# Two attention layers and a mixture of experts: batch 0's tokens sorted by expert, and the causal mask of the row maxima moved to VectorE

## The chip, the core and the metric

The kernel runs on one core of a Trainium2 chip. The metric is the device time of one execution in microseconds (us), the median of several. The engines are named as the profile names them: PE is TensorE (PEld its weight loads), DVE is VectorE, ACT is ScalarE, POOL is GpSimd, SP is SyncE, which issues most of the DMAs. PSUM is the memory that PE writes to, in 8 banks of 128 rows x 512 float32 columns.

## The reference

Input x is (2, 1024, 128) in float32: 2 batches of 1024 tokens, in the kernel 16 tiles of 128 tokens, 8 per batch. Cut to what matters:

```python
x = layernorm(x + attention8(x))         # 8 heads of 16, causal, plus a rank-1 term per head in the scores
n = rmsnorm(x); x = x + mla_attention16(n)   # 16 heads of 8, rotated q and k, keys/values from a 64-wide latent, causal
n = rmsnorm(x)
top = argmax(n @ gate_w.T + gate_b)      # one of 4 experts per token
h = relu(n @ W1[e].T + b1[e])            # 128 -> 512, computed for all e
y = h @ W2[e].T + b2[e]                  # 512 -> 128
x = x + y[top]                           # the chosen expert's result alone
out = layernorm(x)
```

## The kernel before

**Attention** runs in 12 groups of 4 heads: groups 0 to 3 are layer 0 (two per batch), 4 to 11 are layer 1 (four per batch). Keys and queries of a group are bf16 products stacked along the rows. For layer 0 a head uses all 128 rows of the array; for layer 1 it uses 64, and heads 0, 1 and 2, 3 lie in different halves, so that matmuls of the two halves can run at once. A softmax needs each row's maximum before its exponentials, so scores are computed twice. First, for the maxima, with queries as output rows: `MAXES` lists 40 units per group, each a row block i against up to 512 keys, one head, or two where they fit in one bank. `maxima` (L1156) writes a unit to one of 3 banks in a ring (`MAXN`), and DVE reduces the bank to one maximum per row (L1604), after which PE may use it again. 24 of the 40 units hold the diagonal. For these PE first writes the mask into the last 128 columns of each head: a matmul of an identity with a tile of 0 and -1e30 (L1178 in layer 0; L1184 and L1186, 128 and 64 columns wide, in layer 1), and then adds the scores to it (L1189). The maxima are combined, transposed, split into three bf16 parts (L1485 to L1500) and carried by SP into the last rows of the queries (L967, L973), so that the second pass of scores (L1210), with keys as output rows, has the maximum subtracted in it. ACT takes the exponential (L1382), POOL zeroes what lies above the diagonal (L1083, 8 times per group), PE multiplies by the values in float32 (L1227), with 4 buffers of probabilities (`PSLOTS`). A group has 40 units of exponentials too.

**Experts.** A block is 512 tokens, (b, i) with i = 0, 1. After layer 1's attention of a block come the normalised tokens `hat` (L1136), their transpose `feat` (L1394), the gate and `pick` (L1566), which leaves a one-hot row per token. Then all 4 experts are computed for all tokens: 16 `hidden` matmuls of 512 columns (L1362), a `relu` each (L1458), 4 bias matmuls (L1302), 64 `expert` matmuls of 128 columns (L1306), and DVE adds each expert's result times the one-hot column (L1685). All in float32; the profile records each float32 matmul as two. A block thus has 32 records of L1362 and 128 of L1306.

**The order of work** is made once by a planner in Python (`order`, L507). Every step has a wanted position in units of groups (`FIRST`, `BETWEEN`, `READY`, `EXPERTS`, `RESULTS`, L269 to L273), a list of what it needs (`needs`), and costs on each engine (`COSTS`, L312). The planner emits one list, `SCHEDULE`, and each engine runs its own steps of it in that order, in order. Batch 0's two expert blocks are wanted at positions 7.9 to 11.4, beside attention groups 8 to 11; batch 1's at 11.6 to 14.0, for the most part after attention. POOL's and SP's DMAs stand in the same order: a wait in front of one holds what follows on that queue.

## Time and profile before

| | |
|---|---|
| median of 3 runs | 613.81 us (613.73 to 614.38) |
| the profiled execution | 617.44 us |
| its span, first to last instruction | 615.7 us |
| mean granted clock of PE | 0.955 of full speed |
| DMA | 25.64 MB, mean 42 GB/s |

The page says how long each engine was busy in the profiled execution, which chain of work ended last, and which groups of instructions cost most. In its slices the granted clock of PE dips several times in the first half (to 0.5 in a stretch) and stays at nine tenths or more from about 310 us to almost the end. A busy PE is not PE at its peak: matmuls overlap, and the end of one is modelled. So durations of a matmul are longer than the distance from one to the next.

In the rows of a stretch the columns are: start and end in us, length, then busy us and instructions in parentheses for PE, PEld, DVE, ACT, POOL (or for the one engine asked for), then PE's granted clock, the DMA engines' mean busy share and GB/s. In the rows of a group of instructions: line, engine, operation, output<-inputs, shapes, count | busy us, mean ns of one | idle us of the engine before them, and who ended it. In the rows of the timeline: start us, us to the end of the last, engine, line, operation, shapes, and how many were merged.

### The profile page before, as it was taken

How to read it: one execution, taken by the hardware profiler on the slowest of the kernel's cores; microseconds unless marked ns; L12 is line 12 of the kernel's file. 1: busy time of each engine (PE TensorE's matmuls, PEld its weight loads, DVE VectorE, ACT ScalarE, POOL GpSimd, SP SyncE). 2: the span in 40 equal slices, each digit the busy share in tenths (PEclk: the TensorE clock that was granted, in tenths of full speed). 3: DMA queues.
4: the chain of work that ended last, by engine and by line, in shares of the span. 5: the costliest groups of instructions: out<-in, count | busy, mean ns of one | idle time of the engine just before them, and what ended most of it. 6: DMA issues, size and time to landing. Idle time of an engine off the chain costs nothing.

```text
span 615.7 us, 10700 instructions
## 1 busy us (share of the span) xinstructions
PE 549.5 (89%) x3869; PEld 255.0 (41%) x3885; DVE 416.2 (68%) x1063; ACT 350.7 (57%) x673; POOL 157.3 (26%) x217
## 2 busy tenths in 40 slices
PE   6577799888899988898989999999999999999993
PEld 3323234434433333332333334543545445347662
DVE  4396989768888869786878887776666721643144
ACT  4413267754765767745767776656556666653330
POOL 9631012353534155342111221301101102201000
PEclk9877899997999999996989999999999999999998
DMA  3992023005022001020010101001000000010000
GB/s 117 178 210 91 21 70 104 2 1 200 17 71 62 1 25 56 26 79 28 2 54 2 53 2 54 2 2 53 2 3 2 1 2 1 2 35 2 0 15 20
DMA packets 27846, 25.64 MB, mean 42 GB/s; under 512 B 7377, under 2 KB 24401, under 8 KB 27538
## 3 DMA queue, kind: packets, MB, share of 16 engines
q1 hardware_dynamic: 27410, 24.17, 14.4%
q0 software_dynamic: 384, 0.79, 0.7%
q8 instruction: 31, 0.51, 0.3%
q14 instruction: 21, 0.17, 0.1%
HBM read 17.30 MB, written 7.34 MB: 40 GB/s over the span
## 4 chain that ended last, share of the span: by engine, by line
PE 69%; DVE 8%; SPq 8%; ACT 7%; DMA 3%; issue 3%; POOL 1%; DVEq 0%; ACTq 0%; POOLq 0%
PE ps L1227 15%; PE ps L1210 12%; PE ps L1306 10%; PE ps L1362 10%; PE ps L1189 9%; ACT pr L1382 5%; DVE mparts L1604 4%; SPq L913 4%; PE ps L1292 3%; SPq L967 2%; PE ps L1286 2%; DMA qs<-nparts 2%; PE ps L1238 2%; PE ps L1267 2%; PE ps L1184 1%
## 5 line engine op out<-in xcount | busy, mean ns | idle before, releaser
L1382 ACT ACTIVATE pr<-ps 128x512 f32<-128x512 f32 (+1 forms) x480 | 249.9, 554 | 167.1 <-PE ps L1210 137.0
L1604 DVE TENSOR_REDUCE mparts<-ps 128x1 f32<-128x512 f32 (+3 forms) x480 | 279.9, 630 | 89.1 <-PE ps L1189 87.5
L1210 PE MATMUL ps<-qs,ks 64*128 64x512 bf16 (+7 forms) x560 | 153.3, 338 | 18.3 <-ACT pr L1382 10.1
L1189 PE MATMUL ps<-ks,qs 61*128 61x512 bf16 (+7 forms) x576 | 155.4, 347 | 6.9 <-DMA qs<-nparts 3.7
L1227 PE MATMUL ps<-pr,vs 128*32 128x512 f32 (+3 forms) x1152 | 125.0, 507 | 1.5 <-ACT pr L1382 0.3
L1083 POOL TENSOR_SCALAR_AFFINE_SELECT pr<-pr 128x512 f32<-128x512 f32 x96 | 60.9, 634 | 227.7 <-ACT pr L1382 227.6
L1210 PEld LDWEIGHTS ps<-qs,ks 64*128 64x128 bf16 (+1 forms) x576 | 44.6, 96 | 136.9 <-ACT pr L1382 97.5
L1306 PE MATMUL ps<-w,work 128*128 128x128 f32 x512 | 67.7, 283 | 0.0
L1189 PEld LDWEIGHTS ps<-ks,qs 61*128 61x128 bf16 (+1 forms) x576 | 51.0, 100 | 37.8 <-DVE mparts L1604 19.6
L1362 PE MATMUL ps<-feat,w 128*128 128x512 f32 x128 | 65.8, 621 | 0.0
L1306 PEld LDWEIGHTS ps<-w,work 128*128 128x128 f32 x512 | 60.2, 191 | 9.5 <-issue 9.3
L1458 ACT ACTIVATE work<-ps,b 128x512 f32<-128x512 f32 x64 | 43.6, 687 | 32.2 <-PE ps L1362 31.6
L1227 PEld LDWEIGHTS ps<-pr,vs 128*32 128x32 f32 x1152 | 23.0, 108 | 38.6 <-issue 30.2
L1178 PE MATMUL ps<-cmask,identb 128*128 128x128 bf16 (+1 forms) x96 | 25.2, 264 | 14.5 <-DMA ks<-scr0k 6.6
L1685 DVE SCALAR_TENSOR_TENSOR xn<-ps,onehot,xn 128x128 f32<-128x128 f32 x48 | 13.5, 343 | 25.8 <-PE ps L1306 25.8
L1507 DVE RECIPROCAL rc<-ps 128x16 f32<-128x16 f32 x24 | 6.0, 251 | 35.7 <-PE ps L1238 35.7
L1362 PEld LDWEIGHTS ps<-feat,w 128*128 128x128 f32 x128 | 20.6, 189 | 17.6 <-issue 14.8
L1184 PE MATMUL ps<-cmaskx,identx 64*128 64x128 bf16 (+1 forms) x96 | 23.5, 245 | 0.8 <-DVE mparts L1604 0.7
L1184 PE MATMUL ps<-cmask,identb 64*128 64x128 bf16 (+1 forms) x96 | 23.4, 244 | 0.8 <-DVE att L1511 0.4
L1077 POOL COPY vs<-vall 128x256 f32<-128x256 f32 (+1 forms) x12 | 6.0, 502 | 69.5 <-PE ps L1227 69.4
L1178 PEld LDWEIGHTS ps<-cmask,identb 128*128 128x128 bf16 x96 | 9.9, 104 | 31.9 <-DVE mparts L1604 21.8
L1186 PE MATMUL ps<-cmaskx,identx 64*128 64x64 bf16 (+1 forms) x96 | 19.3, 201 | 0.0
(138 smaller groups left out, 501.3 us busy)
## 6 DMA issues: line engine op xcount, KB each, us to landing
qs<-scr0q SPq DMA_DIRECT2D x48, 64.0 KB, 2.3
qs<-scr1q SPq DMA_DIRECT2D x84, 32.0 KB
ks<-scr1k SPq DMA_DIRECT2D x84, 32.0 KB
ks<-scr0k SPq DMA_DIRECT2D x36, 64.0 KB, 2.2
scr0q<-parts SPq DMA_DIRECT2D x4, 384.0 KB, 2.9
scr0k<-parts SPq DMA_DIRECT2D x4, 384.0 KB, 3.8
scr1q<-parts SPq DMA_DIRECT2D x4, 384.0 KB, 2.6
scr1k<-parts SPq DMA_DIRECT2D x4, 384.0 KB, 2.6
```

Source lines behind the costliest of these rows:

```text
L913: queue.dma_start(to, src.rearrange("(h d) t -> d h t", d=at.hd)).then_inc(k_first[half] if (F, k) == (0, 1) else qk_in[F % SLOTS][half % ...
L1083: pool.affine_select(out=p, in_=p, compare_op=ALU.is_ge, fill=0.0, base=0, pattern=[[0, HG], [1, P]], channel_multiplier=-1).then_inc(done ...
L1178: pe.matmul(bank[:, :, w - P:w], identb[:, :], cmask[:, 0:nh, :], start=True, stop=False, skip_group_check=True)
L1184: pe.matmul(bank[:, :, w - P:w], low[0][own, :], low[1][own, 0:nh, :], start=True, stop=False, skip_group_check=True)
L1189: last = pe.matmul(bank[:, h, :], queries(F, 0, h0 + h, i * P, P), keys(F, 0, h0 + h, 512 * c, w), start=not diagonal, stop=True, skip_gro ...
L1210: last = pe.matmul(to[:, h, :], keys(F, 3, h0 + h, j * P, P), queries(F, 3, h0 + h, qb * 512 + lo, n), start=True, stop=True)
L1227: last = pe.matmul(ps[VW * h:VW * (h + 1), PVB, lo:lo + n], vs[:, F % VSLOTS, j, VW * h:VW * (h + 1)], pr[:, st % PSLOTS, h, 0:n], start=( ...
L1306: last = pe.matmul(to, hid[:, e % 2, c, t * P:(t + 1) * P], w2[:, e * HC + c, :], start=False, stop=(c == HC - 1), skip_group_check=True)
L1362: pe.matmul(side(*step), w1[:, c * P:(c + 1) * P], feat[:, columns(b, i)], start=True, stop=True).then_inc(done["hidden"], 1)
L1382: act.activation(pr[:, st % PSLOTS, h0:h0 + nh, 0:STEPS[st][3]], scores_at(F, v), ACT.Exp, scale=GROUPS[F][0].scale).then_inc(exped, 1)
L1458: act.activation(hid[:, c // HC % 2, c % HC, :], side("hidden", b, i, c), ACT.Relu, bias=b1[:, c:c + 1]).then_inc(done["relu"], 1)
L1604: dve.tensor_reduce(mparts[:, F % SLOTS, h0:h0 + nh, i, c], maxes_at(F, u), AX_X, ALU.max).then_inc(taken, 1)
```

## The change

Two edits are made together.

**Sorted tokens.** For batch 0 (`SORTED = [(0, (0, 1))]`) the dense expert steps are gone. PE ranks the tokens: a matmul with a strict lower-triangle matrix, and 8 with a matrix of ones, count for each token and expert how many came before (`rank`). DVE turns the counts into a place for each token, such that each expert's tokens start at a multiple of 128 (`places`); 1024 tokens and 4 experts need at most eleven tiles of 128. POOL scatters the 8 tiles of `hat` to these places in DRAM by indirect DMA (`scatter`), SP loads them back in pieces of four tiles (`sorted`). For each of the eleven tiles POOL fetches the weights of its expert with two indirect DMAs, 128 rows of 640 and of 516 floats (`fetch`), into two pairs of buffers that earlier steps have left free (`parts`, `cos`, `sin`); PE transposes the tile, ACT copies and scales it (`row_turn`, `row_feat`), PE makes the 4 hidden matmuls of 128 columns, ACT 4 relus of 128 columns, PE 4 output matmuls, DVE adds the bias, and SP stores the tile (`tile_hidden`, `tile_relu`, `tile_out`, `tile_sum`, `tile_store`). Then POOL gathers the tokens' rows by 8 indirect DMAs (`collect`) and DVE adds them to the residual (`collected`, one add of 512 columns per block). Batch 1 stays dense.

**The mask.** PE's mask matmuls and their tiles are gone (`identb`, `identx`, the second mask tile). DVE adds a 512-column mask tile, whose last 128 columns hold the triangle, and takes the maximum in one instruction, `tensor_tensor_reduce`, for each head of a diagonal unit, with the masked scores written back to the bank. Units without the diagonal are reduced as before.

```diff
+SORTED = [(0, (0, 1))]
+PIECES = 4
+def by_rows(s):
+    n, J = len(tokens_of(s)), rows_of_tiles(s)
+    out = [("rank", s), ("places", s)] + [("scatter", s, t) for t in range(n)]
+    out += [("fetch", s, j, w) for j in range(2) for w in range(2)]
+    out += [("sorted", s, p) for p in range(-(-J // PIECES))]
+    for j in range(J):
+        out += [("row_turn", s, j), ("row_feat", s, j), ("tile_hidden", s, j), ("tile_relu", s, j), ("tile_out", s, j),
+                ("tile_sum", s, j), ("tile_store", s, j)]
+        if j + 2 < J:
+            out += [("fetch", s, j + 2, w) for w in range(2)]
+    out += [("collect", s, t) for t in range(n)]
+    return out + [("collected", SORTED[s][0], i) for i in SORTED[s][1]]
...
-            add("result", spread(experts(b, i), *EXPERTS[b][i]))
+            if (b, i) in DENSE:
+                add("result", spread(experts(b, i), *EXPERTS[b][i]))
+    for s in range(len(SORTED)):
+        add("rows", spread(by_rows(s), *BY_ROWS[s]))
+BY_ROWS = [(8.45, 11.5)]
...
-        masked = (512 * c + w == (i + 1) * P) * nh * (128 if GROUPS[step[1]][0].n == 0 else 192)
-        return [(PE, (masked + nh * w) / 2400 + 0.01 * nh), (DVE, 0.1 + nh * w / 880)]
+        reads = nh if 512 * c + w == (i + 1) * P else 1
+        return [(PE, nh * w / 2400 + 0.01 * nh), (DVE, 0.1 * reads + nh * w / 880)]
...
+                any_rows = a["x"].rearrange("b t c -> (b t) c")[0:P * (TB + E - 1), :]
+                sp.dma_start(rows_in_order[:, :], any_rows).then_inc(rows_set, 16)
...
+            def scatter(s, t):
+                if t == 0:
+                    pool.wait_ge(rows_set, 32)
+                    pool.wait_ge(done["places"], nth("places", s))
+                b, blocks = SORTED[s]
+                pool.wait_ge(done["hat"], nth("hat", b, blocks[t // 4]))
+                pool.indirect_dma_start(rows_in_order[:, :], IndirectOffsetOnAxis(ap=place_of[:, t:t + 1], axis=0),
+                                        xn[:, tokens_of(s)[t], :], None).then_inc(scattered, 16)
+            def fetch(s, j, w):
...
+                if j >= 2 and w == 0:
+                    pool.wait_ge(done["tile_sum"], nth("tile_sum", s, j - 2))
+                to = (cos, sin)[j % 2][:, 0:w2_row] if w else fetched_w1[:, j % 2 * w1_row:(j % 2 + 1) * w1_row]
+                pool.indirect_dma_start(to, None, a[("w1_rows", "w2_rows")[w]],
+                                        IndirectOffsetOnAxis(ap=row_of[:, j:j + 1], axis=0)).then_inc(fetched[j % 2], 16)
...
-                diagonal = 512 * c + w == (i + 1) * P
-                if diagonal and GROUPS[F][0].n == 0:
-                    pe.matmul(bank[:, :, w - P:w], identb[:, :], cmask[:, 0:nh, :], start=True, stop=False,
-                              skip_group_check=True)
-                elif diagonal:
...
                 for h in range(nh):
                     last = pe.matmul(bank[:, h, :], queries(F, 0, h0 + h, i * P, P),
                                      keys(F, 0, h0 + h, 512 * c, w),
-                                     start=not diagonal, stop=True, skip_group_check=True)
+                                     start=True, stop=True)
...
+                elif kind == "tile_hidden":
+                    s, j = args
+                    pe.wait_ge(done["row_feat"], nth("row_feat", s, j))
+                    pe.wait_ge(fetched[j % 2], 32 * (j // 2 + 1))
+                    wait_bank(*step)
+                    for c in range(HC):
+                        first = j % 2 * w1_row + c * P
+                        last = pe.matmul(side(*step)[:, c * P:(c + 1) * P], fetched_w1[:, first:first + P], tile_x[:, j % 2, :],
+                                         start=True, stop=True)
...
-                    dve.tensor_reduce(mparts[:, F % SLOTS, h0:h0 + nh, i, c], maxes_at(F, u),
-                                      AX_X, ALU.max).then_inc(taken, 1)
+                    bank, to = maxes_at(F, u), mparts[:, F % SLOTS, h0:h0 + nh, i, c]
+                    if 512 * c + w < (i + 1) * P:
+                        last = dve.tensor_reduce(to, bank, AX_X, ALU.max)
+                    else:
+                        for h in range(nh):
+                            last = dve.tensor_tensor_reduce(bank[:, h, :], bank[:, h, :], cmask[:, 512 - w:512], 1.0, -3.0e38,
+                                                            ALU.add, ALU.max, to[:, h:h + 1])
+                    last.then_inc(taken, 1)
```

## Rows read from the trace of the kernel before

**Rows 1.** the page, part 1: busy time of each engine, its share, instructions
```profile
PE 549.5 (89%) x3869; PEld 255.0 (41%) x3885; DVE 416.2 (68%) x1063; ACT 350.7 (57%) x673; POOL 157.3 (26%) x217
```

**Rows 2.** the page, part 4: the chain that ended last, by line
```profile
PE ps L1227 15%; PE ps L1210 12%; PE ps L1306 10%; PE ps L1362 10%; PE ps L1189 9%; ACT pr L1382 5%; DVE mparts L1604 4%; SPq L913 4%; PE ps L1292 3%; SPq L967 2%; PE ps L1286 2%; DMA qs<-nparts 2%; PE ps L1238 2%; PE ps L1267 2%; PE ps L11
```

**Rows 3.** busy time of each engine by stretch; stretches are attention groups 5, 6, 9, 11
```profile
280.60:310.50 29.90, 26.85 (x237) 9.79 (x235) 23.75 (x46) 20.87 (x42) 5.07 (x8) 0.89 0.03 9
...
310.50:340.20 29.70, 27.62 (x250) 9.96 (x249) 24.33 (x49) 21.02 (x42) 5.51 (x9) 0.94 0.10 28
...
417.20:463.80 46.60, 46.60 (x355) 21.24 (x355) 29.77 (x62) 27.17 (x51) 5.51 (x9) 1.00 0.06 18
...
506.60:541.80 35.20, 33.35 (x239) 15.90 (x240) 14.45 (x67) 24.52 (x48) 7.38 (x10) 1.00 0.03 9
```

**Rows 4.** the same view: stretch A, stretch B, tail
```profile
50.00:340.20 290.20, 259.21 (x1878) 104.92 (x1891) 236.00 (x571) 181.14 (x361) 91.18 (x118) 0.94 0.15 46
...
340.20:541.80 201.60, 196.30 (x1512) 90.91 (x1511) 128.68 (x323) 131.34 (x252) 33.96 (x50) 1.00 0.05 15
...
541.80:615.70 73.90, 64.26 (x362) 42.88 (x360) 26.10 (x123) 23.45 (x36) 2.31 (x2) 0.97 0.04 12
```

**Rows 5.** who waited for whom in stretch A: us in total, times, longest
```profile
DVE mparts L1604 <- PE ps L1189: 46.2, 62, 3.8
```

**Rows 6.** timeline of TensorE in the tail: start us, us, instruction, count
```profile
545.46 0.59 PE L1362 MATMUL ps<-feat,w 128*128 128x512 f32 x1
...
546.30 2.94 PE L1306 MATMUL ps<-w,work 128*128 128x128 f32 x24
...
555.00 1.88 PE L1362 MATMUL ps<-feat,w 128*128 128x512 f32 x4
```

**Rows 7.** timeline in group 9: mask matmuls of one diagonal unit
```profile
441.67 0.22 PE L1184 MATMUL ps<-cmask,identb 64*128 64x128 bf16 x1
...
441.73 0.19 PE L1186 MATMUL ps<-cmaskx,identx 64*128 64x64 bf16 x1
```

**Rows 8.** instruction groups of ACT and DVE, whole trace
```profile
L1458 ACT ACTIVATE work<-ps,b 128x512 f32<-128x512 f32 x64 | 43.6, 687 | 32.2 <-PE ps L1362 31.6
...
L1430 ACT COPY work<-ps 128x256 f32<-128x256 f32 x4 | 1.5, 370 | 1.2 <-PE ps L1292 1.2
...
L1443 ACT ACTIVATE work<-work,shift,rstd 128x64 f32<-128x64 f32 x16 | 5.7, 436 | 0.0
...
L1685 DVE SCALAR_TENSOR_TENSOR xn<-ps,onehot,xn 128x128 f32<-128x128 f32 x48 | 13.5, 343 | 25.8 <-PE ps L1306 25.8
```

**Rows 9.** instruction groups by shape, whole trace, L1604
```profile
L1604 DVE TENSOR_REDUCE mparts<-ps 128x2 f32<-128x512 f32 x48 | 32.3, 685 | 8.2 <-PE ps L1189 8.0
...
L1604 DVE TENSOR_REDUCE mparts<-ps 128x2 f32<-128x256 f32 x48 | 18.7, 419 | 10.9 <-PE ps L1189 10.7
```

**Rows 10.** DVE in the timeline, back to back, and a group of small operations
```profile
308.14 1.89 DVE L1604 TENSOR_REDUCE mparts<-ps 128x1 f32<-128x512 f32 x3 [0.80 <-PE ps L1189]
...
541.52 0.38 DVE L1519 BATCH_NORM_AGGREGATE mv<-stats 128x2 f32<-128x6 f32 x4
...
L1546 DVE SCALAR_TENSOR_TENSOR rstd<-rstd 128x4 f32<-128x4 f32 (+1 forms) x48 | 7.8, 163 | 1.6
```

**Rows 11.** POOL's DMA and longest operation; landings of two DMAs
```profile
L913 POOL DMA_DIRECT2D ks<-scr0k x12 | 6.3, 531 | 8.1 <-DMA scr0k<-parts 7.8 <-POOL qs L1031 0.3
...
L1031 POOL MEMSET qs<- 32x2048 f32 x3 | 5.4, 1809 | 0.0
...
ks<-scr0k POOLq DMA_DIRECT2D x12, 64.0 KB, 4.2
...
w<-in_W2T SPq DMA_DIRECT2D x1, 1024.0 KB, 6.9
```

**Rows 12.** DVE in L1604 alone, stretches A and B
```profile
50.00:340.20 290.20, 176.65 (x306) 0.94 0.15 46
...
340.20:541.80 201.60, 90.12 (x150) 1.00 0.05 15
```

312 lines of the change are left out of this document (251 added, 61 removed).

## The prediction

> **What bounds the kernel now.** I read the page's busy shares first. TensorE is busy for 549.5 of 615.7 us, DVE for 416.2, ACT for 350.7 [rows 1]: one engine leads, but a busy TensorE is not yet a bound. The chain that ended last says the same in another way [rows 2]: its five largest parts are TensorE's, and both expert matmuls (L1306 and L1362) are among them with 10% each.
>
> Then I cut the time at the first exponential of each attention group. Groups 5 and 6, which have no expert work beside them, take 29.9 and 29.7 us; group 9, with the same attention work and batch 0's experts, takes 46.6 us with TensorE busy for all of it, DVE for 64% [rows 3]. So in the last third the experts set the pace. In groups 5 and 6 no engine is full: TensorE 0.93, DVE 0.82, ACT 0.71 of group 6. They hold each other up in turns. In the first long stretch TensorE is at 0.89, DVE at 0.81; in the second at 0.97 and 0.64; the tail after attention is batch 1's experts [rows 4]. The waits of the first stretch go both ways: DVE waits 46.2 us for the matmuls of the maxima [rows 5], and TensorE cannot write a fourth bank of maxima before DVE has read the first.
>
> **The sum is by stretch**: opening (to 50 us), A (50 to 340.2), B (340.2 to 541.8), tail (73.9 us). The profiled execution took 617.44 us, 3.6 more than the median 613.81.
>
> **Batch 0's dense experts go, from B.** Consecutive records of L1362 start 0.43 us apart ((1.88 - 0.59) / 3, with 0.59 for the last one alone), those of L1306 0.115 us ((2.94 - 0.29) / 23) [rows 6]. Half of the 128 and 512 records are batch 0's, and 8 bias matmuls of 512 bf16 columns, for which I take four times the 128-column one of rows 7: 64 x 0.43 = 27.5, 256 x 0.115 = 29.4, 8 x 0.24 = 1.9, together 58.8 us. **The eleven tiles come**: each has 4 hidden and 4 output matmuls of 128 columns, 16 records at 0.115 = 1.84, and one transpose, priced like one such record: 11 x 1.95 = 21.5; the rank's 9 short matmuls add 0.7. Net on TensorE: -36.6 us.
>
> **ACT**: 32 relus of 0.687 go (22.0 us). 44 relus and 11 copies of 128 columns come. No row has 128 columns out of PSUM with a pointer operand; a 256-column PSUM copy takes 0.370, a 64-column form with pointers 0.436 [rows 8]. I take 0.40: 22.0 us, net 0 (bounds -2 and +2). **DVE**: 32 pick-ups of 0.343, overlapping, are 9 us; new are 11 tile sums like them, two 512-column adds, priced like a reduction (0.685) [rows 9], and about 15 small operations at 0.163 [rows 10]: 3.8 + 1.4 + 2.4 = 7.6 us, net -1.4.
>
> **POOL and the queues.** POOL gets 38 indirect DMAs: 8 scatters, 22 fetches, 8 gathers. The nearest row, a plain POOL DMA, takes 0.53 us to issue and 4.2 us to land [rows 11]. At 0.53 they cost 20 us of POOL, which is busy for only 34 us of B [rows 4]; the upper bound I take is 1.8 us, as long as POOL's longest memset [rows 11]. A mask queued behind a fetch pair is 1 to 3.6 us late, which the four buffers of probabilities cover mostly: four steps ahead, ACT goes on. SP gets 3 loads and 11 stores in B, and in A, behind the expert weights, a small constant and a 0.7 MB copy that fills the sorted rows once; POOL trades the mask's second tiles for two all-ones tiles, which is even; a store waits for its tile sum, and the maxima's rows queue behind it on SP. The plan makes maxima a group ahead, so that wait is covered by some 30 us. The wait of a fetch is on the tile sum two tiles earlier, so a pair of tiles needs two issues 1.1 + landing 4.2 + hidden 0.9 + relus 1.6 + output 0.9 + sum 0.3 = 9 us, some 12 with queueing. 5.5 pairs are 66 us and the plan spreads them over three groups, 90 us. Cost 0; the cover is B's length.
>
> **The mask leaves TensorE.** In the timeline a 128-column mask matmul occupies 0.06 us up to the next; the 64-column one, half as wide, I take at 0.03 [rows 7]. A group has 16 one-head and 8 two-head diagonal units. Layer 0's groups save 16 x 0.06 + 8 x 0.12 = 1.9 us; layer 1's save 16 x 0.09 + 8 x 0.18 = 2.9, or half where the two halves of the array overlap: I take 2.1. A has 306 of the 480 reductions, 7.65 groups (3.6 of them layer 0's), B 150, 3.75 groups [rows 12]: 15.4 us and 8 us of TensorE.
>
> **It arrives on DVE.** The new instruction reads PSUM once, as the reduction does. Two heads that were one 512-column reduction (685 ns) become two of 256: the columns cost the same (685 - 419 for 256 columns is 1.04 ns each) [rows 9], and an additional instruction costs 0.07 us, since three 512-column reductions take 1.89, 0.60 apart, of which the columns are 0.53 [rows 10]. 8 more per group: 0.56 us. Unknown is what it costs to write the maximum out of an instruction whose output is the whole masked row. From below it is free; from above it is a small dependent operation (0.163 each); nearest is the aggregate that writes two values a row, 4 in 0.38 us, so 0.07 apart [rows 10]. I take 0.07, for all 32 of a group: 2.24. Together 2.8 us per group: A +21.4, B +10.5, opening (the other 24 units) +1.7. That the output goes back into PSUM has no row; I add nothing and keep it in the range.
>
> The Trainium skill (VectorE: DVE Perf Modes, section Two Vector instructions with no wait between them) says that an operation that also writes its accumulator is two instructions. By that the free readout is out. A free readout would leave DVE 26 us lighter over the kernel and my time some 8 us lower. No row of this kernel shows it.
>
> **What becomes of it.** A: TensorE 259.2 - 15.4 = 243.8, DVE 236.0 + 21.4 = 257.4, ACT 181.1. The three busy shares add to 2.33 in A now; at the same packing A takes 682.3 / 2.33 = 293 us, +2 to 3. The mask is a wash there: DVE goes to 0.88 and is late next. B: TensorE 196.3 - 36.6 - 8 = 151.7, DVE 128.7 - 1.4 + 10.5 = 137.8, ACT 131.3, sum 420.8. Groups 5 and 6 pack 2.39 and 2.46; at 2.42 B takes 174 us. A second way, by its five groups: four at 30.5 (groups 5 and 6 take 29.8 now, DVE 24 of it, and 27 then), 26 for the last, which has no maxima (ACT alone 24.5 of busy time there [rows 3]), and 12 for that part of the tiles' 22 us that finds no gap: 160. I take 168, between the two, a gain of 33.5. Opening +1.5. Tail 0: the same experts of batch 1, nothing moved. Sum -33.5 + 2 + 1.5 = -30: 587.4 on the profiled execution, **584** on the median.
>
> **Rivals.**
> 1. *The readout is dear (slower).* Place: DVE in every diagonal unit. At 0.17 a piece a group costs DVE 6.0 us more. With DVE at 0.90 at best (0.82 is the most in rows 3, with TensorE ahead of it there): A is (236 + 46) / 0.9 = 313, +23; B is (128.7 - 1.4 - 14.5 + 22.5) / 0.9 + 35 = 185, where the last group's 14.5 us of DVE and its 35 us stand apart [rows 3], -16; opening +4. Net +10: 624. It decides from 0.145 us per readout on. Against it: the aggregate's 0.07. Chance 0.09.
> 2. *Fetched rows arrive late.* At 1.8 us an issue and 6.9 us a landing, which the largest weight load shows [rows 11], a pair takes 14, with queueing 20, 5.5 pairs 111 us against 90; TensorE waits in order before hidden matmuls: 20 us lost, 604. Chance 0.11.
> 3. *TensorE's clock falls.* It was at 1.00 of the full 2.4 GHz all through B, where TensorE never rested, and at 0.89 in group 5, where it idled for 10% [rows 3]; that is a fifth of the time at 1.2 GHz. With B at 0.89, 152 us of TensorE become 171, and at the packing above (19 / 2.42) 8 us are lost: 592. Chance 0.12. The Trainium skill (TensorE: Matmul & The Clock Gate, Part 1) has the throttled clock as the default that activity lifts, so it speaks against thinning out TensorE's work; by it the time would be this 592.
> 4. *TensorE alone counts.* Then DVE's additions hide: A loses its 15.4 at the share 0.89, -13, B is 152 / 0.97 = 156, -46: 555. Against it DVE's 0.82 in groups 5 and 6. Chance 0.08.
> 5. *The change does not do what it says*: TensorE's time goes, but the dense experts only filled gaps that now stay open (613). Groups 5 and 6, 17 us shorter than group 9 on the same attention work, speak against it. Chance 0.03.
>
> **The numbers.** The forecast has 0.57, with 568 to 600 of its own. Left out are rival 1 above and rival 4 below, 0.17 together; with the bounds of ACT, of PSUM writing and of packing the range is 562 to 607. Faster: 0.57 + 0.11 + 0.12 + 0.08 = 0.88; same (0.2%, 1.2 us, about what a measurement here tells) 0.03; slower 0.09.
>
> **What would show it.** Right: groups 8 to 10 at 29 to 34 us; TensorE under 0.92 in B; DVE near 0.85 to 0.9 in A and B; A within 4 us of 290; a tail of 74 us; a second DVE record of about 0.07 us behind each masked maximum. Wrong: A longer by over 10 us, long waits of TensorE for fetched rows, POOL busy for over 80 us of B, or groups 8 to 10 still over 38 us.

## The result, and the profile after

The changed kernel takes 624.58 us (median of 4 runs, 622.28 to 626.78) against 614.04 before on the same chip: ratio 1.0164, 95% interval 1.0132 to 1.0196, slower by 1.6%. Forecast were 584 us, with a range of 562 to 607. Some executions of a kernel are slower for reasons outside it; the ratios here leave them out, the medians do not. The profiled execution took 624.46 us, its span is 622.5. The page's part 1 of the changed kernel, beside [rows 1]:

```profile
PE 524.9 (84%) x3258; PEld 219.3 (35%) x3273; DVE 436.6 (70%) x1538; ACT 343.3 (55%) x696; POOL 193.6 (31%) x252
```

TensorE's records did become fewer by 611 and its busy time shorter by 24.6 us; DVE gained 20.4 us. The time did not follow. Stretches A, B and tail of the changed kernel, cut at the same first exponentials as [rows 4], same columns:

```profile
48.20:347.40 299.20, 261.71 (x1598) 93.29 (x1610) 252.11 (x870) 180.40 (x361) 93.03 (x124) 0.90 0.15 47
347.40:548.60 201.20, 170.07 (x1203) 70.05 (x1201) 130.71 (x454) 124.74 (x275) 70.38 (x87) 0.89 0.21 59
548.60:622.50 73.90, 64.22 (x361) 42.84 (x359) 26.45 (x126) 23.53 (x35) 2.31 (x2) 0.95 0.04 11
```

A is 9.0 us longer than before, and B is as long as before (201.2 and 201.6). The tail is the same 73.9, and the opening is 1.8 us shorter (1.5 more were forecast). PE's granted clock is 0.90 and 0.89 where it was 0.94 and 1.00. Groups 5, 6 and 8 to 11 one by one, beside [rows 3] (group 7, left out, takes 35.5 us):

```profile
282.20:313.40 31.20, 27.34 (x199) 8.01 (x197) 25.50 (x85) 20.74 (x42) 5.53 (x9) 0.90 0.02 4
313.40:347.40 34.00, 29.81 (x204) 8.83 (x201) 26.67 (x89) 21.09 (x42) 5.53 (x9) 0.85 0.09 25
...
382.90:436.40 53.50, 38.44 (x246) 12.91 (x244) 38.93 (x139) 23.39 (x46) 19.54 (x23) 0.76 0.27 74
436.40:477.60 41.20, 40.87 (x304) 20.55 (x308) 32.81 (x107) 28.62 (x73) 14.57 (x18) 0.93 0.29 82
477.60:513.10 35.50, 32.76 (x258) 16.28 (x250) 16.29 (x48) 26.87 (x67) 13.13 (x17) 1.00 0.28 78
513.10:548.60 35.50, 27.74 (x179) 9.78 (x180) 13.55 (x57) 23.32 (x47) 15.29 (x18) 0.90 0.09 25
```

Groups 9 and 10 did become shorter, 41.2 and 35.5 us where they were 46.6 and 42.8. Group 8 gives most of it back, 53.5 where it was 43.6, and group 7 another 2.1. Group 8 holds one long stop, 21.5 us in which ACT has a single instruction; the window of the stop alone:

```profile
414.90:436.40 21.50, 10.08 (x36) 2.74 (x36) 12.27 (x49) 0.59 (x1) 8.22 (x10) 0.57 0.51 141
```

PE is busy for less than half of it, at a granted clock of 0.57 (most of the time at 1.2 of 2.4 GHz), and the DMA engines are at 0.51 against 0.05 over B before [rows 4]: this is where rows are scattered and weights fetched. The chain through it (start us, us, what):

```profile
416.12 0.59 DVE ps L1851
416.71 0.06 DVE mparts L1851
416.77 5.55 another core or an unknown queue
422.34 0.70 DVE ps L1851
```

DVE waits 5.55 us for a signal that the program takes from PE's matmul of the maxima and the profile finds no sender for. That line is taken up below. The masked maximum and POOL's indirect transfers, as groups of the changed kernel:

```profile
L1851 DVE CUSTOM_DVE_ANT_0 ps<-ps,cmask 128x384 f32<-128x384 f32 x96 | 52.3, 580 | 7.8 <-PE ps L1344 7.3
L1851 DVE DVE_READ_ACCUMULATOR2_ANT mparts<- 128x1 f32 x384 | 53.3, 139 | 0.0
...
L1223 POOL DMA_INDIRECT rows_in_order<-xn,place_of x8 | 7.9, 985 | 8.5 <-issue 8.5
```

### The profile page after: what moved, and what is told of

It is laid out like the page before. It is cut to its first block, busy times and chain, and to the rows that moved or that the text cites. A ratio compares the mean times of both kernels' runs of the same rounds, so it can differ in the third digit from the quotient of the medians.

```text
span 622.5 us, 10067 instructions
## 1 busy us (share of the span) xinstructions
PE 524.9 (84%) x3258; PEld 219.3 (35%) x3273; DVE 436.6 (70%) x1538; ACT 343.3 (55%) x696; POOL 193.6 (31%) x252
## 4 chain that ended last, share of the span: by engine, by line
PE 59%; DVE 14%; ACT 9%; SPq 8%; issue 4%; DMA 3%; POOL 2%; another core or an unknown queue 1%; DVEq 0%; ACTq 0%; POOLq 0%
PE ps L1382 14%; PE ps L1365 13%; PE ps L1344 9%; ACT pr L1574 6%; DVE ps L1851 5%; PE ps L1461 5%; PE ps L1517 4%; SPq L1028 4%; PE ps L1447 3%; SPq L1098 2%; PE ps L1441 2%; PE ps L1393 2%; DVE mparts L1848 2%; PE ps L1547 2%; DMA qs<-nparts 2%
## 5 line engine op out<-in xcount | busy, mean ns | idle before, releaser
L1851 DVE CUSTOM_DVE_ANT_0 ps<-ps,cmask 128x384 f32<-128x384 f32 (+3 forms) x384 | 178.5, 515 | 38.7 <-PE ps L1344 30.6
L1848 DVE TENSOR_REDUCE mparts<-ps 128x1 f32<-128x512 f32 x192 | 124.5, 685 | 35.1 <-PE ps L1344 34.4
L1851 DVE DVE_READ_ACCUMULATOR2_ANT mparts<- 128x1 f32 x384 | 53.3, 139 | 0.0
L1669 ACT ACTIVATE work<-ps,b 128x512 f32<-128x512 f32 x32 | 21.9, 686 | 28.9 <-PE ps L1517 28.4
L1461 PE MATMUL ps<-w,work 128*128 128x128 f32 x256 | 31.0, 279 | 0.0
L1517 PE MATMUL ps<-feat,w 128*128 128x512 f32 x64 | 30.1, 600 | 0.2 <-DVEq L1792 0.2
L1461 PEld LDWEIGHTS ps<-w,work 128*128 128x128 f32 x256 | 29.3, 192 | 2.7 <-issue 2.7
L1579 ACT COPY ot<-ps 128x512 f32<-128x512 f32 x24 | 14.1, 587 | 15.7 <-PE ps L1382 9.6
L1393 PE MATMUL ps<-ident,ot 128*128 128x128 f32 x96 | 18.3, 322 | 2.4 <-DVE mparts L1848 1.7
L1196 POOL COPY vs<-vall 128x256 f32<-128x256 f32 (+1 forms) x12 | 6.1, 506 | 43.0 <-PE ps L1382 42.8
L1291 POOL TENSOR_TENSOR parts<-work,parts 128x512 bf16<-128x512 f32 x12 | 13.9, 1161 | 6.6 <-ACT parts L1603 6.5
```

Of the source, the lines that this page charges most:

```text
L1393: last = pe.transpose(bank[:, t * P:(t + 1) * P], ot[:, q, t * P:(t + 1) * P], ident[:, :])
L1461: last = pe.matmul(to, hid[:, e % 2, c, t * P:(t + 1) * P], w2[:, e * HC + c, :], start=False, stop=(c == HC - 1), skip_group_check=True)
L1517: pe.matmul(side(*step), w1[:, c * P:(c + 1) * P], feat[:, columns(b, i)], start=True, stop=True).then_inc(done["hidden"], 1)
L1669: act.activation(hid[:, c // HC % 2, c % HC, :], side("hidden", b, i, c), ACT.Relu, bias=b1[:, c:c + 1]).then_inc(done["relu"], 1)
L1848: last = dve.tensor_reduce(to, bank, AX_X, ALU.max)
L1851: last = dve.tensor_tensor_reduce(bank[:, h, :], bank[:, h, :], cmask[:, 512 - w:512], 1.0, -3.0e38, ALU.add, ALU.max, to[:, h:h + 1])
```

## The experiments

Eighteen runs were made, one of them a repeat. The table has each one's median, its ratio to before, the four parts of its profiled execution (opening to the first exponential not shown), and the stop of the exponentials ahead of group 9. The parts come from one execution each, which can lie some us from the median (plan_of_mask 632.02 against 628.07, held 607.42 against 611.80, mask_old_order 618.92 against 616.71), so differences of a part of 1 or 2 us say little. The medians of before were 613.9 to 614.6 us beside the experiments.

"Late" counts PE's semaphore signals, some 1300 in a trace, for which the next recorded event comes over 0.4 us after the end of the instruction's record. It mixes two things. In the ten traces with 14 or more, 37 to 62 semaphore events of PE, DVE and ACT are missing from the trace (at most 7 in the other ten), and where an event is missing the next one counts; DVE and ACT together have 21 to 38 such signals there. But part of the lateness needs no event to be seen: in the same ten traces, after the first scatter, DVE starts four to six maxima over 0.4 us later than both its own last instruction and the matmuls of that bank had ended, and the latest of a trace 1.3 to 9 us later. In the other ten no such start is over 0.6 us late. So the column tells two kinds of execution apart; it is not a number of delays.

| kernel | us | ratio (95%) | groups 0-4 | 5-7 | 8-11 | tail | stop | late |
|---|---|---|---|---|---|---|---|---|
| before | 614.04 | | 230.7 | 92.9 | 168.3 | 73.9 | 0.7 | 0 |
| after | 624.58 | 1.0164 (1.0132-1.0196) | 234.0 | 100.7 | 165.7 | 73.9 | 21.6 | 21 |
| mask_alone | 622.88 | 1.0121 (1.0061-1.0181) | 235.2 | 98.5 | 165.5 | 73.9 | 1.0 | 0 |
| plan_of_mask | 628.07 | 1.0200 (1.0155-1.0245) | 234.6 | 102.4 | 170.0 | 74.0 | 0.4 | 1 |
| mask_old_order | 616.71 | 1.0028 (0.9992-1.0065) | 234.7 | 94.8 | 165.6 | 73.9 | 1.1 | 0 |
| no_mask | 616.95 | 1.0037 (1.0001-1.0073) | 229.1 | 101.3 | 163.4 | 73.9 | 17.6 | 1 |
| warm | 624.47 | 1.0149 (1.0092-1.0206) | 234.3 | 100.2 | 166.4 | 73.9 | 17.7 | 0 |
| whole_old_cost | 623.51 | 1.0140 (1.0051-1.0228) | 233.6 | 94.1 | 171.2 | 74.2 | 20.6 | 26 |
| sort_alone | 613.60 | 0.9978 (0.9945-1.0010) | 229.4 | 92.9 | 166.9 | 74.2 | 17.8 | 0 |
| sort_again | 618.36 | 1.0069 (1.0040-1.0098) | 230.7 | 93.0 | 173.3 | 74.2 | 21.7 | 24 |
| sort_plain | 605.28 | 0.9838 (0.9784-0.9892) | 231.0 | 93.0 | 159.4 | 74.2 | 15.1 | 0 |
| masks_first | 613.06 | 0.9954 (0.9915-0.9993) | 230.8 | 92.0 | 161.1 | 77.8 | 21.8 | 32 |
| rows_first | 613.17 | 0.9961 (0.9931-0.9991) | 230.2 | 92.9 | 167.7 | 74.0 | 17.3 | 34 |
| both_late | 606.17 | 0.9852 (0.9808-0.9896) | 230.3 | 93.1 | 160.4 | 71.7 | 17.3 | 25 |
| ahead | 615.26 | 1.0007 (0.9982-1.0032) | 229.9 | 98.9 | 158.2 | 80.1 | 8.8 | 23 |
| held | 611.80 | 0.9964 (0.9918-1.0009) | 228.4 | 92.1 | 164.7 | 71.4 | 8.3 | 30 |
| plain_fetch | 603.10 | 0.9823 (0.9776-0.9869) | 230.2 | 92.9 | 156.7 | 71.7 | 14.6 | 14 |
| plain_all | 599.88 | 0.9768 (0.9689-0.9847) | 230.9 | 92.0 | 154.1 | 71.7 | 10.7 | 0 |
| mask_both_late | 605.81 | 0.9795 (0.9740-0.9849) | 232.4 | 94.4 | 159.6 | 71.7 | 13.4 | 22 |
| no_experts | 580.86 | 0.9440 (0.9332-0.9547) | 231.0 | 93.1 | 134.4 | 73.9 | 9.4 | 1 |

### One half of the change at a time

mask_alone turns the sorting off. sort_alone puts the mask back on TensorE, and the planner's old cost of a maximum with it.

```diff
-SORTED = [(0, (0, 1))]
+SORTED = []
```

> The masked maximum on DVE alone; the experts of both batches stay dense. In the changed kernel stretch A (the first seven groups of exponentials) grew from 290 to 299 us although DVE's work there grew only by 16 us, as forecast. If the mask edit alone costs that (DVE's added work, or TensorE's clock, 0.90 there against 0.94), this kernel takes 622 to 630 us, A 295 to 302 and the clock in A 0.90. If the loss of A is owed to the sorted tokens (their loads, their 0.7 MB copy, the order planned around them), it takes 610 to 616 us and A is at 290.

> The sorted tokens alone; the mask stays a matmul on TensorE. If the mask edit is what cost, and the sorted tiles gain as forecast, this takes 580 to 592 us. If the queues and the indirect DMAs hold the engines up (group 8 took 53.5 us in the changed kernel, with 10 us in which TensorE stood still), it takes 600 to 612 us, group 8 again over 45 us. If the clock gives the gain of B back, B's clock is under 0.93 here too and the time 595 to 605.

The mask's move, with the new cost in the planner, loses 1.2%, and the sort, priced at 33.5 us, gives nothing. The same sort kernel, run again on another chip (sort_again, below), even lost 0.7%. The halves add up: 1.0121 times 0.9978 or 1.0069 is 1.010 to 1.019, around the 1.0164 of both. So there are two errors to find, one in each half.

### The mask: work, relief or order

warm lets TensorE write as many dummy columns as the mask had, into columns that the scores overwrite; no_mask leaves the mask out wholly (plain reductions), so its maxima are those of unmasked rows.

```diff
+                if 512 * c + w == (i + 1) * P:
+                    pe.matmul(bank[:, :, w - P:w], cmask[:, 0:P], pair, start=True, stop=True, skip_group_check=True)
```

> The changed kernel, order and all, with TensorE also doing matmuls of the mask's size where the mask stood, which the scores then overwrite: TensorE has its old work back, DVE keeps the new. If TensorE's relief only lowered its clock, this is no slower than the changed kernel (618 to 626 us) and the clock in A returns from 0.90 to 0.93 or more. If TensorE's relief was worth its size (15 us in A, 8 in B by the forecast), it is 10 us or more slower, 634 or more.

> The changed kernel, order and all, with plain maxima everywhere and no mask in them at all, on no engine (the row maxima are then taken over all keys of the units read). DVE is back at its old work. If DVE's added work is what holds the changed kernel, this gains most of it, 25 us or more: under 600. If the stalls of the sorted tiles and the clock hold it, it gains under 12 us: 612 to 624.

warm has TensorE's old columns back and is as slow as the change. In groups 0 to 7 it takes 334.5 us against 334.7, with the clock of A at 0.92 in place of 0.90: there TensorE's relief was worth nothing, whatever share of that the lower clock has. For groups 8 to 11 the pair cannot tell, since after's trace has late signals and warm's has none; without the stop warm takes 148.7 us there and after 144.1. no_mask takes back 7.6 us, of which 4.9 in groups 0 to 4 (229.1 against 234.0); groups 5 to 7 stay at 101.3, so DVE's new instructions are not what lengthens those. What is left is the order. plan_of_mask is the kernel before with only this edit, and mask_old_order is mask_alone with this edit undone:

```diff
-        masked = (512 * c + w == (i + 1) * P) * nh * (128 if GROUPS[step[1]][0].n == 0 else 192)
-        return [(PE, (masked + nh * w) / 2400 + 0.01 * nh), (DVE, 0.1 + nh * w / 880)]
+        reads = nh if 512 * c + w == (i + 1) * P else 1
+        return [(PE, nh * w / 2400 + 0.01 * nh), (DVE, 0.1 * reads + nh * w / 880)]
```

> Edit: the kernel of before, with one thing of the change alone, the planner's cost of a maximum (no mask columns on TensorE, 0.1 us for each readout on DVE); the mask stays on TensorE and nothing is sorted. The kernel with the mask's move alone took 622.9 us against 614.5, 8.3 more. The theory that DVE's added instructions cost this expects the same within 0.5% of before here, 612 to 617 us, with groups 0 to 4 as long as before (45.4, 49.5, 45.5, 36.0, 54.3 us). The rival, that the order which the planner makes with the new costs loses part of it, expects 617 to 620 us, with groups 2 to 4 together 3 us longer than the 135.8 of before.

> Edit: the mask added by DVE as in the change, nothing sorted, but the planner keeps its costs of a maximum from the kernel before, so that the order of the steps is that of before (but for the small step that built TensorE's masks). The change's order alone, with the mask still on TensorE, took 628.1 us, and with the mask on DVE 622.9. The theory that the order is what costs, and the mask's move by itself gains a little, expects 606 to 611 us, with groups 0 to 4 at or below the 231 us of before. The rival, that DVE's added instructions cost some 8 us where they stand (the kernel without any mask in the change's order took 617.0), expects 617 to 622 us.

My theory said that DVE's work costs and the order does not; it fell. The same instructions in the new order lose 2.0%, 13.7 us, more than the whole change. The stretches of groups 5, 6 and 7 in plan_of_mask (before they took 92.9 together; 5 and 6 are in [rows 3]):

```profile
283.80:315.90 32.10, 28.96 (x246) 10.97 (x245) 23.79 (x46) 20.99 (x41) 5.51 (x9) 0.87 0.03 8
315.90:351.40 35.50, 32.61 (x253) 12.00 (x250) 25.02 (x49) 21.30 (x43) 5.51 (x9) 0.81 0.09 24
351.40:386.20 34.80, 32.67 (x262) 13.75 (x260) 27.70 (x68) 23.36 (x46) 7.82 (x11) 0.90 0.09 25
```

In group 6, 5.8 us longer than before, the work of ACT is that of before (21.30 us busy, 21.02 before) and TensorE's columns are too. TensorE is busy for 32.61 us in place of 27.62, at a clock of 0.81 in place of 0.94. Busy time times clock is nearly the same, 26.4 and 26.0, and its idle time grew from 2.1 to 2.9 us only. So there the lower clock makes up most of the length. How the order brings the clock down is not shown. In the old order the mask's move takes 1.0028, no change that can be told: groups 0 to 4 are 4.0 us longer and groups 5 to 7 1.9, and 8 to 11 are 2.7 shorter, in one execution each.

whole_old_cost, the full change with the old cost, was to confirm it:

> Edit: the whole change as it is (624.6 us), with the planner's cost of a maximum taken from the kernel before; no other step is moved by hand. The mask's move alone took 622.9 us with the new cost and 616.7 with the old one. If the new cost loses as much in the whole change, this takes 613 to 618 us, with groups 0 to 4 together at 231 to 235 us in place of 233.9 and groups 5 to 7 at 94 to 96 in place of 100.8; if the sort's stops at the ends of groups 8 and 11 outweigh it, 619 to 625 us.

It does so only in part. Groups 5 to 7 return to 94.1 us, 6.6 less than after, but groups 8 to 11 take 5.5 us more. Group 11 alone makes 5.0 of it (40.5 against 35.5): with the old cost eight transfers of POOL stand in one piece there, as in sort_alone (below), and with the new cost a mask comes in between. An error of the order in one place was traded for one in another.

### The sort: what could be had

no_experts is sort_alone without the ranking, the transfers and the tiles: batch 0's experts are left out.

> Edit: the kernel with the sort alone (613.6 us), without the ranking, the scatters, the fetches, the eleven tiles and the collects: it leaves out batch 0's experts wholly. Groups 8 to 11 take 168.2 us in before and 166.8 in the sort alone. The theory that the sort's own work and its queues take back the gain expects 138 to 148 us for the four groups here, by the planner's order with the maxima of group 9 finished in time, and 583 to 592 us in all. The rival, that these groups are bound by something that neither the experts nor the tiles touch (the maxima on DVE and their rows, or TensorE at its lower clock), expects 155 to 165 us for them and 600 to 611 us.

```profile
373.80:419.60 45.80, 38.74 (x293) 16.29 (x291) 34.80 (x81) 23.65 (x46) 7.79 (x11) 0.82 0.10 28
419.60:450.00 30.40, 27.29 (x237) 9.94 (x235) 23.85 (x46) 20.64 (x41) 5.10 (x8) 0.88 0.05 13
450.00:478.30 28.30, 24.86 (x211) 8.29 (x209) 19.11 (x38) 21.00 (x43) 5.53 (x9) 1.00 0.01 2
478.30:508.30 30.00, 26.15 (x179) 9.26 (x179) 12.44 (x59) 22.79 (x46) 7.41 (x10) 1.00 0.03 10
```

These are groups 8 to 11 without any expert work: 134.4 us, so batch 0's dense experts cost 33.9 us of before, as groups 5 and 6 had promised. The sort as it was built takes 32.5 us (166.9 - 134.4) for work that I had priced at 12. The gain was there, and the sort's own work, transfers and queues spend it.

### Where it is spent: three queues

In sort_alone the chain between group 8's last exponential (403.7) and group 9's first (421.5) is on SP (start us, us, what). L1023 is a load of group 11, L1071 of sorted rows, L1101 a row of maxima of group 9, and the DMA line is the landing of the last such row:

```profile
411.03 0.30 SPq L1023
411.43 0.38 SPq L1071
411.86 0.51 SPq L1071
412.40 0.50 SPq L1071
412.95 0.51 SPq L1101
...
415.40 0.59 SPq L1101
416.03 4.74 DMA qs<-nparts
420.81 0.60 PE ps L1402
```

At the end of group 11, POOL in sort_alone (timeline: start us, us, engine, line, instruction):

```profile
505.44 0.95 POOL L1264 DMA_INDIRECT xn<-rows_out,place_of  x1 [0.15 <-issue]
506.69 0.94 POOL L1264 DMA_INDIRECT xn<-rows_out,place_of  x1 [0.30 <-issue]
...
514.18 0.94 POOL L1264 DMA_INDIRECT xn<-rows_out,place_of  x1 [0.30 <-issue]
515.14 2.85 POOL L1221 TENSOR_SCALAR_AFFINE_SELECT pr<-pr 128x512 f32<-128x512 f32 x4
```

Eight collects (the gathers of the finished rows) stand in a row, 1.25 us apart, and four diagonal masks that TensorE waits for come behind them at once. masks_first holds the collects behind the masks, rows_first puts group 9's rows ahead of the loads; both_late has both and a later start.

```diff
-    return [("tile_store", s, k) for k in range(J)]
+    return [("tile_store", s, k) for k in range(J)] + [("mask", NF - 1, k) for k in range(8)]
...
-        return [("scatter", s, t) for t in range(n)] + [("lo", 15)]
+        return [("scatter", s, t) for t in range(n)] + [("lo", 15), ("rows", 9, 2)]
...
+        if F == NF - 1:
+            out.append(("rows", 9, 2))
...
-BY_ROWS = [(8.45, 11.5)]
+BY_ROWS = [(9.1, 12.0)]
```

> Edit: the kernel with the sort alone (613.6 us), where POOL's eight collects of the finished rows are held back until the eight diagonal masks of group 11 are done. In the sort alone, POOL issues them from 505.4 to 515.1 us, 1.25 us apart, and the next mask on POOL comes at 515.1; TensorE stands still for 5.4 us and the exponentials for 6.6. The theory that POOL's queue holds the masks up expects no gap there, group 11 at 35 to 36 us in place of 40.0, and 608 to 610 us, if the collects do not become late themselves in the tail (they would then lengthen the tail from 73.9 us). The rival, that this stop is the indirect transfers' traffic or the clock, expects group 11 to stay at 39 to 40 us and the time at 612 to 615.

> Edit: the kernel with the sort alone (613.6 us), where on SP's queue the 24 loads of group 11 and the three loads of sorted rows stand behind the six rows of maxima of group 9, not ahead of them. In the sort alone, the combine of group 9 is at 406.5 us, SP issues its rows at 413.0 and they land at 420.8, with the exponentials idle from 403.7 to 421.5. The theory of SP's queue expects the rows issued at about 409 and landed by 414 to 417, group 8 at 44 to 47 us in place of 50.7, and 608 to 611 us. The rival, that the maxima are late by themselves and the landings slow because of the rows that are scattered and fetched, expects the rows to land less than 2 us earlier and 612 to 615 us.

> Edit: the kernel with the sort alone (613.6 us), with both edits (collects behind group 11's masks; group 9's rows ahead of the loads on SP) and the stream of the sort placed from group 9.1 to 12.0 in place of 8.45 to 11.5, so that its scatters and fetches do not stand beside the end of group 8. If stops at the ends of groups 8 and 11 are what took back the gain of the sort, this comes to 602 to 607 us, with the four groups 8 to 11 at 152 to 158 us together in place of 166.8. If the gain is lost to the lower clock of TensorE, which falls as its work becomes less, the four groups stay above 162 us and the time above 610.

masks_first shows POOL's queue: group 11 falls from 40.0 to 31.3 us. The collects are then late themselves, the tail grows by 3.6, and the stop ahead of group 9 was 4.0 longer in this execution, so the time hardly moves. rows_first is a miss: the rows were issued at 417.2 us and not at 409, since the maxima themselves came later, and the stop stayed at 17.3. Both executions had late signals and sort_alone's had none, which spoils the comparison. Against sort_again, which had them too, the stop is 4.4 us shorter, but DVE's late starts also add up to 3.6 us less there (7.2 and 10.8), so that what SP's queue costs is not shown. both_late gains 8.2 us on before, with groups 8 to 11 at 160.4, between the two theories, and its stop is still 17.3 us. Its later start of the sort is in it too, and was not run alone.

### The stop: order, bytes or indirect transfers

ahead asks for group 9's maxima 1.4 groups early in place of 1.2 (`MAX_AHEAD`); held lets the ranking wait for group 9's rows; plain_fetch and plain_all replace the 22 fetches, or all 38 indirect transfers, by plain ones of the same bytes (all tiles then use the same weights, and in plain_all rows are not sorted).

```diff
-                pool.indirect_dma_start(to, None, a[("w1_rows", "w2_rows")[w]],
-                                        IndirectOffsetOnAxis(ap=row_of[:, j:j + 1], axis=0)).then_inc(fetched[j % 2], 16)
+                pool.dma_start(to, a[("w1_rows", "w2_rows")[w]][0:P, :]).then_inc(fetched[j % 2], 16)
...
-        return [("pick", SORTED[a[0]][0], i) for i in SORTED[a[0]][1]] + [("rank_made",)]
+        return [("pick", SORTED[a[0]][0], i) for i in SORTED[a[0]][1]] + [("rank_made",), ("rows", 9, 2)]
```

> Edit: the same version (606.2 us), with the maxima of group 9 wanted 1.4 groups ahead of it in place of 1.2. In that version the last of them is computed behind all 40 pairs of scores of group 8, at 406.5 us with the exponentials of group 8 done at 403.5, and the exponentials then wait 17.3 us. The theory that the place of the maxima in the order is what keeps the gap expects the gap at 6 us or less and groups 7 and 8 together 5 to 9 us shorter than their 81.7, in all 598 to 602 us. The rival, that the work of the maxima is only moved into group 7 and lengthens it by as much, expects groups 7 and 8 within 2 us of 81.7 and 604 to 608 us.

> Edit: the same version (606.2 us), with the ranking of the sort held until the rows of group 9's maxima are issued, so that neither DVE's placing nor a scatter nor a fetch stands beside the end of group 8. If the sort's own transfers and DVE instructions make the gap of 17.3 us, it comes to 10 us or less, with no signal of TensorE late before 410 us, and group 8 takes 38 to 41 us in place of 48.3; groups 9 and 10 become longer by some 5 us since the tiles start later. If the gap is the order of the maxima alone, it stays at 13 us or more and group 8 at 45 or more. In all 603 to 610 us.

> Edit: the last version with the mask on TensorE (606.2 us), where each of the 22 fetches of weights is a plain transfer of the first 128 rows in place of an indirect one of as many rows of the same length: the same bytes, no addresses from a tile. It leaves out the choice of the rows, so every tile uses the same weights. Under the theory that the indirect transfers hold up TensorE's signals (25 of 1313 come over 0.4 us late there, none in before, and the exponentials wait 17.3 us at the end of group 8) it expects fewer than 8 late ones, a gap of 12 us or less, and 596 to 602 us. The rival, that it is the bytes and their landing in SBUF or only the order of the maxima, expects as many late ones, the gap at 16 to 18 us and 604 to 607 us.

> Edit: the version with the mask on TensorE and both queues mended (606.2 us), where all 38 indirect transfers (8 scatters, 22 fetches, 8 collects) are plain ones of the same size. It leaves out the sorting of the rows and the choice of the weights. With the fetches alone made plain it took 603.1 us, 14 signals of TensorE came over 0.4 us late in place of 25, and the gap was 14.6 us. If indirect transfers hold up the signals, here fewer than 4 are late, and the time is 598 to 602 us; if the bytes do, as many as 14 stay late and it takes 602 to 605 us. The gap at the end of group 8 is expected at 12 us or more under both, since the maxima's place in the order is unchanged.

ahead, against both_late: the stop falls to 8.8 us, but groups 5 to 7 grow by 5.8, two new stops of 4.9 and 5.2 us stand in group 9 and the tail takes 80.1: the work was moved. held: the stop falls to 8.3 and group 8 to 40.4 us, as expected of the sort's transfers; the scatters and fetches then stand in group 9, which takes 49.3. The median of 611.80, on another chip, is 5.6 us over both_late's and above the 603 to 610 expected. In both places they stop something.

plain_all gains 6.3 us on both_late (1.0%, on another chip, and the intervals of the two ratios overlap a little), no signal is late in place of 25, and the stop is 10.7 us. plain_fetch lies between, with 14 late. The pair of timelines at that stop, first both_late (indirect), DVE and TensorE at the maxima (L1886, L1378):

```profile
410.13 0.63 PE L1383 MATMUL ps<-ks,qs 61*128 61x256 bf16 x2
...
410.99 0.96 POOL L1257 DMA_INDIRECT cos<-in_w_rows,row_of  x1 [0.30 <-issue]
...
412.19 0.51 PE L1383 MATMUL ps<-ks,qs 61*128 61x384 bf16 x1
412.26 0.95 POOL L1257 DMA_INDIRECT parts<-in_w_rows,row_of  x1 [0.30 <-issue]
...
414.35 0.69 DVE L1886 TENSOR_REDUCE mparts<-ps 128x2 f32<-128x512 f32 x1 [1.77 <-remote]
...
415.10 0.29 PE L1378 MATMUL ps<-cmaskx,identx 64*128 64x128 bf16 x1 [2.40 <-issue]
```

and plain_all at the same steps:

```profile
406.97 0.33 PE L1380 MATMUL ps<-ks,qs 61*128 61x384 bf16 x1
...
407.31 3.15 DVE L1883 TENSOR_REDUCE mparts<-ps 128x2 f32<-128x512 f32 x6
...
410.67 1.80 DMA qs<-nparts
```

The two matmuls of 256 columns that start at 410.13 fill the bank of 512 that DVE reads at 414.35. By their records they end at 410.76, and DVE's last instruction before it ends at 412.57: with indirect fetches under way DVE starts 1.8 us after both. TensorE, which has filled its three banks by 412.7, stands until DVE has read one. With plain transfers the same bank is ready at 406.34 and DVE reads it, and five others, in a row from 407.31. The last line is from the chain: the maxima's rows land 1.80 us after their last issue, where they took 4.74 in sort_alone. The kind of transfer does not explain that: in sort_alone the last row is issued 3.2 us after the last of the first four fetches, and in sort_again, the same kernel, 9.5 us after it, and there it lands in 1.79. What stays in plain_all, 10.7 us, is the order: without the dense experts group 8's exponentials end at 402.6, the last maximum of group 9 is only started at 404.1, and combining, issuing and landing its rows takes until 412.5.

One thing did not fit: sort_alone has 38 indirect transfers and none of PE's signals late. The last two runs were for that. sort_plain is sort_alone with all transfers plain, sort_again is sort_alone unchanged.

> Edit: the kernel with the sort alone (613.6 us, none of its signals late in its profiled execution, the rows of group 9's maxima landing 4.74 us after the last issue), with all 38 indirect transfers made plain, of the same bytes. It leaves out the sorting of the rows and the choice of the weights. If indirect transfers cost what they cost in the version with mended queues (606.2 to 599.9), this takes 606 to 609 us, the rows land in 2 to 3 us and the stop of 17.8 us falls to 11 to 14; no signal is late. If the 6.3 us there came from the late signals alone, which this kernel did not show, it takes 611 to 615 us and the landing stays over 4 us.

> Edit: none, the kernel with the sort alone once more. If the late signals belong to the kernel, its trace again shows none or one, with the stop at 17 to 18 us. If they belong to the execution, it may show 20 to 35, with the stop at 17 to 22 us and the rows of maxima waiting for DVE rather than for SP's queue. The time is expected at 612 to 615 us either way.

sort_again shows 24 late signals and takes 618.36 us where sort_alone took 613.60: the late signals belong to the execution or the chip and not to the kernel. The 4.8 us between the two medians are the nearest there is to their price, from two chips and one trace each. The chain at its stop:

```profile
406.76 1.29 DVE mparts L1884 x2
408.05 8.78 another core or an unknown queue
...
416.86 0.70 DVE mparts L1884
```

It is the line of the changed kernel, longer: DVE's wait for a bank of maxima. The matmul of that bank ended at 407.84 by its record.

sort_plain has no late signal, its rows land 1.91 us after the last issue, and it takes 605.28 us. That is 13.1 us under sort_again, beside which it ran on the same chip, and 8.3 under sort_alone, more than I expected (606 to 609); the intervals of the three ratios are apart. So this kernel pays for its indirect transfers even where no signal is late, and more where they are. Of the 7.5 us that groups 8 to 11 are shorter than in sort_alone, 2.7 are in the stop, about what the faster landing gives, and 5.0 in group 11 (35.0 against 40.0). That is POOL's queue again, where eight plain collects take 4.3 us and not 9.7:

```profile
505.54 4.32 POOL L1262 DMA_DIRECT2D xn<-rows_out  x8
```

mask_both_late is the whole change with both_late's edits and the old cost of a maximum:

> Edit: the whole change (sort and mask on DVE), with the planner's old cost of a maximum, and on POOL the collects behind group 11's masks, on SP group 9's rows ahead of the loads, the sort's stream from group 9.1 to 12.0. With the mask on TensorE these edits took 606.2 us. If the mask's move gains what the order had hidden, 596 to 603 us and under both kernels; if DVE's added instructions cost some 8 us, 610 to 616 us.

605.81 us beats both kernels, but its interval and that of both_late overlap; the mask's move adds nothing that these runs can tell.

## Why the prediction was wrong

- **Part B, "-33.5", failed.** B is 0.4 us shorter in the changed kernel and 1.3 in sort_alone, in which the sort stands alone. Three terms of the second way were wrong, and for sort_alone they close: 160 by that way (I took 168), +2.9 for group 7 (33.4 and not 30.5), +16.9 for groups 8 to 11 without expert work (134.4 and not 3 x 30.5 + 26 = 117.5; 9.4 of it is a stop that is there without any sort, and its chain runs over SP's loads of group 11 and the maxima's rows), +20.5 for "12 for that part of the tiles' 22 us that finds no gap" (32.5 in sort_alone; 26.0 with both queues mended, 19.7 with plain transfers as well). Together 200.3, and B of sort_alone is 200.3. The largest is the last: no run shows that the tiles can hide 10 of their 22 us, and with their transfers and queues they took 32.5.
- **"Cost 0" for POOL and the queues failed.** I took between 0.53 and 1.8 us an issue; it is 0.95 and 0.30 between, 1.25 together, and so within my bounds. The mask behind a fetch pair was seen (1 to 3.6 us), but not eight collects in a row, 10 us. On SP I named the queueing of the maxima's rows, and covered it by 30 us of lead. That lead was never there, and the trace of before shows it: the last of group 9's rows is issued at 414.9 us, 2.3 before the group's first exponential at 417.2, and TensorE already waits 0.80 us for it to land.

```profile
411.82 3.67 SPq L967 DMA_DIRECT2D qs<-nparts  x6
...
416.70 0.39 PE L1210 MATMUL ps<-qs,ks 64*128 64x512 bf16 x1 [0.80 <-DMA qs<-nparts]
```

  The sort then made it a stop, since from before to sort_alone the exponentials of group 8 end 12.8 us earlier (416.5 and 403.7) and the last maximum of group 9 starts only 2.2 earlier (407.9 and 405.7).
- **A, "+2", was +9.** The packing of A held (the busy shares add to 2.32, forecast 2.33), and DVE was priced a little high: 252.1 us busy against 257.4 forecast. The term that failed is TensorE's 243.8, which came to 261.7 at a clock of 0.90; its relief was worth nothing in A (warm). The term that was missing is the order: I read the two changed lines of the planner as bookkeeping and gave them none. How the 9.0 us divide depends on the way taken. In the old order the mask's move makes A 5.0 us longer (295.2, from 48.1 to 343.3) and the order adds 4.0. With the mask still on TensorE the order alone adds 12.0 (302.2), and the mask's move then takes 3.0 off.
- **The readout** was about right. DVE in the changed kernel's timeline:

```profile
296.73 0.60 DVE L1851 CUSTOM_DVE_ANT_0 ps<-ps,cmask 128x384 f32<-128x384 f32 x1
297.24 0.14 DVE L1851 DVE_READ_ACCUMULATOR2_ANT mparts<- 128x1 f32 x1
297.24 0.60 DVE L1851 CUSTOM_DVE_ANT_0 ps<-ps,cmask 128x384 f32<-128x384 f32 x1
```

  Masked maxima of 384 columns start 0.51 us apart, 0.40 of it the columns at 1.04 ns, so 0.11 for the additional instruction and its readout together; I had 0.14. The Trainium skill (VectorE: DVE Perf Modes, section Two Vector instructions with no wait between them) has such an operation as two instructions. The trace agrees: two records, of which the second, 0.139 us long where I had named a record of about 0.07, lies beside the next.
- **The rivals.** Rival 1 named 624 us and a slower kernel, which is what came, by luck: its readout of 0.17 is not there. Rival 2's transfers did cost, but TensorE's waits for fetched weights are no item among its waits; the stops are at the maxima, their rows and the masks instead. Rival 3 was right about the clock and about TensorE's busy time in B (171 us named, 170.1 measured), but its 592 us is not what came, since the packing fell as well: the busy shares of B add to 2.12 (425.5 / 201.2), not 2.42. Rivals 4 and 5 are out: the time does not follow TensorE, and no_experts shows that the dense experts did not fill gaps only.
- **The signs I had named**: groups 8 to 10 at 29 to 34 (53.5, 41.2, 35.5: wrong), TensorE under 0.92 in B (0.85: right), DVE 0.85 to 0.9 (0.84 in A, 0.65 in B: wrong in B), A within 4 us (wrong), tail 74 (right). Of the signs against it, groups 8 and 9 over 38 us came (group 10 not); A over 10 us longer (9.0), waits for fetched rows and POOL over 80 us in B (70.4) did not.

## What to carry to other kernels

When work is taken out beside a pipeline, ask first what ran under its cover, and read the lead of the next stage from the trace before, at its last piece and not its first: here it was 2.3 us and not 30, and it is the first thing that comes late. Where a planner orders the work, a changed cost is a change of its own: run the old work in the new order, and price it from that. Count what stands in one piece on each queue, not only its sum, and see who is behind it.

## What was not expected of the hardware

- Indirect transfers on POOL's queue came with late starts of DVE behind TensorE's matmuls. Of thirteen traces with such transfers ten have them, from the first scatter on, the latest of each trace by 1.3 to 9 us; the same ten lack 37 to 62 semaphore events. The seven traces without such transfers have no such start over 0.6 us and lack at most 4, though plain_all and sort_plain move the same bytes. The other three with them (sort_alone, warm, no_mask; at most 7 events missing) have none either. They ran beside each other on one chip, on which three later runs had both. The same kernel ran both ways (sort_alone 613.60 us, sort_again 618.36). What decides it is open, and so is whether the signal or the matmul itself is late, since the ends of matmuls are modelled.
- The landing of the maxima's rows went with what was still under way. Issued 3.0 to 3.4 us after the last of four fetches, the last row landed after 4.58 to 4.88 us (sort_alone 4.74, warm, no_mask); issued 8.7 to 9.6 us after it, beside the same kind of transfers, after 1.72 to 1.79 (after, masks_first, sort_again). In plain_all and sort_plain it took 1.80 and 1.91, 6.6 and 11.5 us after.
- An indirect transfer of 128 rows occupied POOL for 0.94 to 0.99 us with 0.30 before the next, the same for rows of 128 floats and of 640; a plain one in its place took some 0.55.
- The order of the same instructions alone moved the time by 2.0% (13.7 us), with TensorE's granted clock in group 6 at 0.81 in place of 0.94.
